# Graph attention with layer norm: the last stage's sum and final multiply go from VectorE to GpSimd, and half of the scaling from ScalarE to VectorE

## The reference

```
e     = leaky_relu(concat(x[src], x[dst], ef) @ W_attn + b)
m     = concat(x[src], ef) @ W_ne
alpha = softmax of e over the edges of each dst
z     = segment_sum(alpha * m, dst)
y     = x + relu(concat(x, z) @ W_out)
out   = (y - mean(y)) / sqrt(var(y) + 1e-5)      # per row of 64
```

## Time and profile before

| what | value |
|---|---|
| time, median of 3 runs | 4009.97 us (4007.27 to 4010.44) |
| the profiled execution: its time, and its span in the trace | 4021.12 us, 4019.2 us |
| busy: POOL, VectorE, TensorE, ScalarE | 2972.2, 2837.8, 2260.2, 2020.9 us |
| last gather issued by GpSimd, start | 3927.99 us |
| epilogue: first transpose, start | 3955.72 us |
| first output multiply (L801) and last one, start | 3976.30 us, 4015.92 us |
| last output DMA issued | 4016.93 us |

### The profile page before, as it was taken

The page is one execution under the profiler, slowest core; times in us unless marked ns, Lnnn a source line. Parts: engine busy times, 40 slices in busy tenths (PEclk is TensorE's granted clock), DMA queues, the critical chain, the costliest instruction groups (busy, mean ns, idle before and its releaser), DMA issues.

```text
span 4019.2 us, 47762 instructions
## 1 busy us (share of the span) xinstructions
PE 2260.2 (56%) x9822; PEld 2005.2 (50%) x9823; DVE 2837.8 (71%) x5649; ACT 2020.9 (50%) x3433; POOL 2972.2 (74%) x3133
## 2 busy tenths in 40 slices
PE   2666655555555555555555555555555555555556
PEld 1555555544454444454444444544444544454456
DVE  8776666666766767676676766676767676766777
ACT  2665555544454444444444444444444444444446
POOL 7777777777777777777777777777777777777770
PEclk9665556556556565555655555555655556555557
DMA  6655555555555555555555555555555555555542
GB/s 166 177 173 156 159 157 156 160 158 157 158 157 157 157 157 157 157 157 157 158 157 157 157 157 157 157 158 157 157 157 157 157 157 158 157 157 157 158 147 66
DMA packets 409354, 627.14 MB, mean 156 GB/s; under 512 B 208412, under 2 KB 208796, under 8 KB 409332
## 3 DMA queue, kind: packets, MB, share of 16 engines
q1 hardware_dynamic: 296260, 519.51, 40.7%
q0 software_dynamic: 100000, 102.60, 12.3%
q10 hardware_dynamic: 13072, 4.80, 0.6%
HBM read 621.58 MB, written 4.81 MB: 156 GB/s over the span
## 4 chain that ended last, share of the span: by engine, by line
POOL 73%; issue 24%; DVE 1%; PE 1%; POOLq 1%; ACT 0%; DMA 0%; DVEq 0%
POOL V L372 73%; POOLq L390 0%; PE psE L909 0%; POOLq L381 0%; PE psT L902 0%; PE psG L844 0%; DVE y L801 0%; DVE var L782 0%; DMA V<-in_x_dram,srcs 0%; DVE y L778 0%; DVE mean L791 0%; DVE y L798 0%; DVE prod L785 0%; DMA srcs<-in_src_dram 0%; ACT zb L522 0%
## 5 line engine op out<-in xcount | busy, mean ns | idle before, releaser
L372 POOL DMA_INDIRECT V<-in_x_dram,srcs x3125 | 2971.2, 951 | 956.0 <-issue 952.9
L844 PE MATMUL psG<-V,pT 128*128 128x130 f32 x6250 | 1461.4, 427 | 366.6 <-DVE psS L663 366.6
L844 PEld LDWEIGHTS psG<-V,pT 128*128 128x128 f32 x6250 | 1361.5, 330 | 506.1 <-DVE psS L663 506.1
L837 PE MATMUL psT<-ident,e 128*128 128x128 f32 x3125 | 720.8, 404 | 1286.3 <-DVE e L658 1286.3
L448 ACT COPY pT<-psT 128x512 f32<-128x512 f32 x784 | 420.9, 589 | 1714.8 <-PE psT L837 1708.9
L837 PEld LDWEIGHTS psT<-ident,e 128*128 128x128 f32 x3125 | 573.8, 215 | 1392.7 <-DVE e L658 1392.7
L594 DVE TENSOR_TENSOR prod<-V,psM 128x512 f32<-128x512 f32 x782 | 502.4, 684 | 637.6 <-DMA V<-in_x_dram,srcs 621.8
L658 DVE TENSOR_TENSOR e<-zb,psE 128x1024 f32<-128x1024 f32 x392 | 478.8, 1221 | 259.4 <-DVE u L599 162.1
L705 DVE CUSTOM_DVE_ANT_0 um<-ubc,psS 128x1024 f32<-128x1024 f32 x391 | 477.6, 1221 | 20.2 <-ACT psS L461 19.3
L599 DVE TENSOR_REDUCE u<-prod 128x8 f32<-128x1024 f32 x391 | 477.0, 1220 | 13.5
L469 ACT ACTIVATE psE<-um,ebias 128x1024 f32<-128x1024 f32 x391 | 437.2, 1118 | 12.8
(11 more groups left out here) (97 smaller groups left out, 524.7 us busy)
## 6 DMA issues: line engine op xcount, KB each, us to landing
ubc<-scores SPq DMA_DIRECT2D x391, 512.0 KB
dbc<-in_dst_dram SPq DMA_DIRECT2D x390, 512.0 KB, 4.0
V<-in_edge_attr_dram SPq DMA_DIRECT2D x390, 256.0 KB, 2.8
V<-in_x_dram,srcs POOLq DMA_INDIRECT x3125
srcs<-in_src_dram SPq DMA_DIRECT2D x390, 4.0 KB
scores<-u SPq DMA_DIRECT2D x390, 4.0 KB
out_dram<-y SPq DMA_DIRECT2D x12, 256.0 KB
xt<-in_x_dram ACTq DMA_DIRECT2D x6, 448.0 KB, 14.2
```

The source lines that it names most:

```text
L372: nc.gpsimd.indirect_dma_start(Vx[:, s, j, 1:XW], None, x[:, :], bass.IndirectOffsetOnAxis(ap=srcs[:, s, j:j + 1], axis=0)).then_inc(h_in[ ...
L837: last = nc.tensor.transpose(psT[:, i, (j - 4 * i) * P:(j - 4 * i + 1) * P], e1[:, 0:n * P].rearrange("q (p j) -> q j p", j=n)[:, j, :], i ...
L844: last = nc.tensor.matmul(psG[:, 0:AW], pT[:, i, (j - 4 * i) * P:(j - 4 * i + 1) * P], V[:, LEADIN + s * SLOT + XW * j:LEADIN + s * SLOT + ...
```

## The change

GpSimd gets an epilogue of its own. It adds the scaled product to `y0` (new L406, the work of L778) and multiplies each octet by the reciprocal deviation (new L410, the work of L801). Both are tensor-tensor instructions of 128 x 512 with both inputs in SBUF. ScalarE scales four of the eight blocks in place of all eight, and VectorE the other four in one instruction of 128 x 256 (new L801), which reads the product out of PSUM. For that, TensorE writes the second half of an octet's product into a bank of `psS`, where it wrote all of it into `psE`. A new semaphore, `half_ready`, says that VectorE's half is scaled; GpSimd's add and TensorE's next product for the same bank wait for it. VectorE's chain for an octet begins one place later than before, since the add is no longer its own, so `octets` runs three places past the end on VectorE where it ran two.

```
 @block.gpsimd   (new, behind the last gather)
+            pool.wait_ge(y_copied, PAIRS + 2)
+            def octet(o, par):
+                w, w3 = width(o), width(o - 3)
+                if w:
+                    rows = y0[:, 8 * o:8 * o + w, :]
+                    pool.wait_ge(h_ready, o + 3)
+                    pool.wait_ge(half_ready, o + 3)
+                    nc.gpsimd.tensor_tensor(rows, rows, (e1, zb)[par][:, 0:w * F].rearrange("p (b f) -> p b f", f=F), ALU.add).then_inc(o_read, 1)
+                if w3:
+                    blk3 = slice(8 * (o - 3), 8 * (o - 3) + w3)
+                    pool.wait_ge(rstd_done, o - 2)
+                    nc.gpsimd.tensor_tensor(y0[:, blk3, :], y0[:, blk3, :], rstd[:, blk3].unsqueeze(2).broadcast_to((P, w3, F)), ALU.mult).then_inc(rows_ready, 1)
+            octets(octet, 3)
 @block.scalar
-                    for j in range(w1):
+                    for j in range(min(4, w1)):
 @block.vector
+                    dve.wait_ge(o_ready, o + 3)
+                    m = w - 4
+                    if m > 0:
+                        nc.vector.tensor_tensor((e1, zb)[par][:, 4 * F:w * F].rearrange("p (b f) -> p b f", f=F),
+                                                psS[:, par * 512 + 4 * F:par * 512 + w * F].rearrange("p (b f) -> p b f", f=F),
+                                                rl[:, 8 * o + 4:8 * o + w].unsqueeze(2).broadcast_to((P, m, F)), ALU.mult).then_inc(half_ready, 1)
...
-                    nc.vector.tensor_tensor(rows, rows, (e1, zb)[par][:, 0:w * F].rearrange("p (b f) -> p b f", f=F), ALU.add).then_inc(o_read, 1)
...
-                    nc.vector.tensor_tensor(y0[:, blk2, :], y0[:, blk2, :], rstd[:, blk2].unsqueeze(2).broadcast_to((P, w2, F)), ALU.mult).then_inc(rows_ready, 1)
 @block.tensor
+                    pe.wait_ge(half_ready, o)
-                            last = nc.tensor.matmul(psE[:, (1 - par) * 512 + j * F:(1 - par) * 512 + (j + 1) * F], zT[:, 1 - par, j * P:(j + 1) * P],
+                            last = nc.tensor.matmul((psE, psS)[i][:, (1 - par) * 512 + j * F:(1 - par) * 512 + (j + 1) * F], zT[:, 1 - par, j * P:(j + 1) * P],
```

More of the change, by code:

```diff
@@ L214, in graph_attention @@
         h_ready = sem("h_ready")
+        half_ready = sem("half_ready")
         z_turned = sem("z_turned")
@@ L769, in _ @@
             dve.wait_ge(y_copied, PAIRS + 2)
+            dve.sem_inc(half_ready, 2)
+            dve.wait_ge(rl_ready, 1)
             def octet(o, par):
-                w, w1, w2 = width(o), width(o - 1), width(o - 2)
+                w, w1, w2, w3 = width(o), width(o - 1), width(o - 2), width(o - 3)
+                rows1 = y0[:, bass.ds(8 * (o - 1), w1), :] if w1 else None
+                prodv = prod[:, 0:w1 * F].rearrange("p (b f) -> p b f", f=F) if w1 else None
                 if w:
-                    rows = y0[:, bass.ds(8 * o, w), :]
-                    prodv = prod[:, 0:w * F].rearrange("p (b f) -> p b f", f=F)
-                    dve.wait_ge(h_ready, o + 3)
-                    nc.vector.tensor_tensor(rows, rows, (e1, zb)[par][:, 0:w * F].rearrange("p (b f) -> p b f", f=F), ALU.add).then_inc(o_read, 1)
@@ L779, in octet @@
[L779 to L788, removed]
@@ L789, in octet @@
-                if w:
-                    dve.wait_ge(relu_done, o + 1)
-                    nc.vector.tensor_reduce(mean[:, 0:w], prodv, AX, ALU.add).then_inc(sum_done, 1)
+                    dve.wait_ge(o_ready, o + 3)
[4 more added lines that the diff above has]
+                                                rl[:, 8 * o + 4:8 * o + w].unsqueeze(2).broadcast_to((P, m, F)), ALU.mult).then_inc(half_ready, 1)
+                    else:
+                        dve.sem_inc(half_ready, 1)
@@ L792, in octet @@
                 if w2:
                     blk2 = bass.ds(8 * (o - 2), w2)
[L794 to L798, removed]
-                if w2:
-                    dve.wait_ge(rstd_done, o - 1)
-                    nc.vector.tensor_tensor(y0[:, blk2, :], y0[:, blk2, :], rstd[:, blk2].unsqueeze(2).broadcast_to((P, w2, F)), ALU.mult).then_inc(rows_ready, 1)
@@ L803, in _ @@
-            octets(octet, 2)
+                    dve.wait_ge(sq_ready, o - 1)
+                    nc.vector.tensor_reduce(var[:, blk2], ubc[:, par, 0:w2 * F].rearrange("p (b f) -> p b f", f=F), AX, ALU.add).then_inc(sq_summed, 1)
+                if w1:
+                    dve.wait_ge(o_read, o + 2)
+                    nc.vector.scalar_tensor_tensor(prodv, rows1, 0.0, xt[:, bass.ds(8 * (o - 1), w1), 0:F], ALU.max, ALU.add).then_inc(relu_done, 1)
+                if w2:
+                    dve.wait_ge(sq_summed, o - 1)
+                    nc.vector.tensor_scalar(var[:, blk2], var[:, blk2], 1.0 / F, EPS, ALU.mult, ALU.add).then_inc(var_done, 1)
@@ new lines, in octet @@
+                if w1:
+                    dve.wait_ge(relu_done, o)
+                    nc.vector.tensor_reduce(mean[:, 0:w1], prodv, AX, ALU.add).then_inc(sum_done, 1)
+                if w3:
+                    blk3 = bass.ds(8 * (o - 3), w3)
+                    dve.wait_ge(std_ready, o - 2)
+                    nc.vector.reciprocal(rstd[:, blk3], rstd[:, blk3]).then_inc(rstd_done, 1)
+                if w1:
+                    dve.wait_ge(sum_done, o)
+                    nc.vector.scalar_tensor_tensor(rows1, mean[:, 0:w1].unsqueeze(2).broadcast_to((P, w1, F)), -1.0 / F, prodv, ALU.mult, ALU.add).then_inc(cen_done, 1)
```

## The result

The changed kernel takes 4020.11 us (median of 11 runs, 4017.19 to 4022.0), the kernel before 4010.22 us (median of 11, 4007.27 to 4011.55): 9.9 us more, a ratio of 1.0024 (95% interval 1.0015 to 1.0034). That is slower, since the interval leaves out 1, and the loss is five times the 2.0 us of the forecast.

The account below looks back on a forecast made before the run. GpSimd's gathers were taken to bound the untouched edge loop, VectorE the late epilogue and TensorE its low-clock octets. Contention's 1.5 us plus 0.5 at the end, added to the median 4009.97, gave 4012 us, range 4005 to 4020.

Parts of the forecast that it names:

- the forecast itself: Epilogue: VectorE and GpSimd hold each other up in changing order, octets of 3.65 to 4.56 us, 4012 us; chance 0.45.
- slower by over 0.2%: Whole kernel: the outcome given only to the rival with slow GpSimd instructions and its multiply always first; chance 0.21.
- relu first at 3.65 us: Epilogue octet if VectorE's relu precedes GpSimd's multiply: the centring is 0.46 us late, 3.65 us per octet.
- the multiply first at 4.56: Epilogue octet if GpSimd's multiply precedes VectorE's relu: relu waits for all of it, 4.56 us per octet.
- D = 1.2: Assumed time in us of each new GpSimd instruction over 512 columns, the middle of bounds 0.82 and 1.54.
- D = 1.12: Alternative GpSimd instruction time in us, from the Trainium skill's add; said to make the sum about 0.5 us lower.
- ScalarE is not the bound: Epilogue: ScalarE waits 0.55 us per octet for VectorE, so its saved 0.78 us counts only within the loops.
- no contention: Rival: VectorE and GpSimd don't disturb each other in the epilogue, 3.42 us per octet, 4007 us; chance 0.30.
- TensorE's 5.01 us cover every loop above: Epilogue octets before 3985 us, at low clock: TensorE's 5.01 us per octet hide the new loops, so no change.
- SyncE's stores wait for the multiply as before and stay behind it by as much: Program end: output stores follow the last multiply at the old distance, so nothing is added there.
- The one on the other side: Rival: GpSimd's multiply always first and GpSimd slow, D of 1.40 us or more; 4020 us at 1.54; chance 0.21.
- The clock rival: Epilogue: TensorE avoids the low-clock stretch at 0.52, 8.6 us less, 4001 us; chance 0.04.

Follow-up runs that it names:

- e4: The changed kernel with GpSimd's multiply waiting until relu of the octet just added is done; 4016.68 us, ratio 1.0018 to the kernel before.
- e3: The changed kernel with relu reading one operand from PSUM in place of the SBUF input (output differs); 4011.64 us, ratio 1.0009 to the kernel before.
- e5: The changed kernel with the multiply by the reciprocal back on VectorE, so GpSimd only adds; 4018.03 us, ratio 1.0023 to the kernel before.
- e1: The kernel before with GpSimd waiting for the last output multiply, then filling a single column; 4015.4 us, ratio 1.0017.
- e7: The kernel before with GpSimd waiting for the last output multiply and doing nothing after it; 4015.55 us, ratio 1.0016.
- e2: The changed kernel with the last four multiplies and the last two blocks' add on VectorE; 4012.25 us, ratio 1.0011 to the kernel before.
- e10: e8 with ScalarE's square root moved behind its scalings and square, and eight octets on GpSimd in place of nine; 4005.51 us against 4009.0, ratio 0.9994.
- e8: The kernel before with nine octets' multiplies on GpSimd, waiting for relu, and VectorE's two sums put next to each other; 4020.38 us, ratio 1.0024.

## Why the prediction was right in its range and wrong in its size

The 4020.1 us lie at the very end of the range, 4005 to 4020, and not in the 4009 to 4015 of the forecast itself; "slower by over 0.2%" had a chance of 0.21. That end of the range had been worked out for slow instructions on GpSimd, which were not there, so it is luck that it holds the result.

**The loops and the order.** The mechanism is right: VectorE's turn fell, waits took over, and the octet went from 3.88 to 4.13 us. That 4.1 was forecast is luck again. It was the middle of two orders, relu first at 3.65 us and the multiply first at 4.56, and in the changed kernel the multiply began first in all nine full octets that had one, and held relu by more than 0.2 us in six of them. By the forecast's loop for that order, 4.56 us, it was 0.43 faster: the hand-over to GpSimd took 0.07 us in place of 0.25, and from the end of the add to L815 it was 1.48 in place of 1.84, since the multiply took 1.04 in place of 1.2 and relu didn't lose all of it; the add took 1.36 in place of 1.2. The other two figures can be held against runs that force them: 3.72 us with relu first (e4) for 3.65, and 3.53 us with relu not held (e3) for 3.42. Nothing held, add and multiply took 1.27 and 1.04 us, so D = 1.2 was near. (With D = 1.12 the prediction's own formulas give 7 x 1.5 x 0.08 = 0.8 us less, not 0.5.)

What I had overlooked in the rows of before is that the same loop ran there. From add to variance it is 1.80 us, to the square root 0.20, to the scalings 0.12, to their end 1.73, to the next add 0.03: 3.88 us, just VectorE's turn. So each octet was bound twice, though VectorE shows no wait, and "ScalarE is not the bound" was too simple: taking off the multiply (L801), which is no part of this loop, could by these rows give nothing alone. No run tried that on the kernel before. The change shortened the loop's scalings by 0.82 us (1.73 to 0.91) and lengthened the way from add to variance by 1.04 (1.80 to 2.84), with the longer add and the held relu.

**Contention.** It exists: e3 shows it for relu, e4 and e5 for the centring, the add and the multiply. The Trainium skill, SBUF — State Buffer, section "Who interferes with whom", has it that a VectorE instruction with two inputs in SBUF contends with a GpSimd instruction that reads SBUF; the traces agree, 1.38 us for relu beside the multiply and 0.68 with one operand in PSUM. I had given "no contention" a chance of 0.30; that rival fell.

**Before 3985 us.** The step "TensorE's 5.01 us cover every loop above", and with it "no change", was too kind: at full clock the early octets were 3.7 to 4.2 us apart as well (by their transposes, 3955.58 to 3971.41 us), and low-clock stretches came at other places (0.52 from 3971.4 to 3974.7 and from 3982.2 to 3992.3). From the fourth octet's transposes to the last ones' the changed kernel took 2.3 us more than before (38.27 against 35.93), ahead of that 1.1 us more, of which a low clock at the start is a part, and behind it, from the last transposes to the last multiply's end, 1.4 us more where I had put 0.5. In all 4.8 us, against 2.0. How much of the difference is the clock, which fell elsewhere, one trace of each can't say.

**The end.** This is the step that failed. "SyncE's stores wait for the multiply as before and stay behind it by as much" is true, and the span did not end with the stores. I had read that GpSimd did nothing in the epilogue, and not that the end of its program lay there too, hidden; so the sum put it at nothing. It took 5.5 us of the 10.9, and the result without it would have been some 4 us later, at the upper end of the forecast's own case. e1 and e7 give it back with one added wait, e2 takes it away.

**The rivals.** The one on the other side had the time, 4020 us, and the order (multiply first), but not the cause: it needed instructions of 1.4 us or more, and they took 1.04 and 1.27 when nothing held them. What made it slower by over 0.2% was the drain: with the drain hidden, e2, it was 0.11%. The clock rival didn't occur in the changed kernel, which had two stretches at 0.52.

## What to carry to other kernels

Before giving an engine work at the end of a program, look at what the end of its program costs, and when it has to begin to be hidden: here GpSimd had to be done 8.4 us before the last store was, some 5.4 us before the last multiply. Before putting elementwise work on GpSimd beside VectorE, count on each side the instructions with two operands in SBUF; here only beside VectorE's others was it free (e10). And when a step moves off the bound, follow the loop of waits that remains, with the order on every engine, in the kernel before too, since an engine that never waits can have such a loop of the same length beside it: relieving VectorE by some 0.9 us per octet gave a longer octet, and moving one square root in ScalarE's queue was worth 1.4 us per octet (4.85 to 3.47, e8 to e10).

## What was not expected of the hardware

GpSimd's drain at the end of its program took 8.3 to 8.6 us after its last instruction or wait in each trace, whether that was a gather, a multiply, a fill or a wait alone, against 13 ns on SyncE and 0.2 to 1.1 us on the others. Whether it is as long in a program without gathers wasn't tried. A VectorE instruction that GpSimd held ended 0.55 us after the one that held it, 0.13 us short of its own whole length (relu, centring and multiply in the changed kernel, e4 and e5). TensorE's granted clock fell to its lower level at other places in the two traces of before and in the changed kernel, as given above, and in e3 and e10 it stayed at 1.00 until the last products; the longest octet of the changed kernel, 5.45 us from add to add (3986.99 to 3992.44), lies where it was low. That may be a part of the spread of some 5 us between runs, which was not tried.
